# Edge rows of a four-layer graph network put together in DRAM during the attention and loaded in one piece per half chunk, with rows of 268 bytes

## The reference, cut to what matters

```python
h = relu(layernorm(x)); x = x + gnn0(h)   # attention over 4 heads, per edge; sum over dst; projection, norm
h = relu(layernorm(x)); x = x + cheb(h)   # two Chebyshev layers of order 3, rows summed by src
h = relu(layernorm(x)); x = x + gine(h)   # see below
h = relu(layernorm(x)); x = x + gat(h)    # softmax over the edges of each dst

def gine(node_feats):                      # edge_feats = edge_attr_64
    message = relu(node_feats[dst] + edge_feats)
    message_reduce = segment_sum(message, src, 3125)
    return mlp((1 + eps) * node_feats + message_reduce)
```

## Time and profile before

| | us |
|---|---|
| median of 3 runs | 3534.71 |
| lowest and highest run | 3491.54, 3550.27 |
| span of the profiled execution | 3529.8 |
| POOL busy in the 800 scatters (L1254) | 818.6 |
| first and last scatter start | 1576.7, 2938.6 |

### The profile page before, as it was taken

One profiled execution on the slowest core, in us unless ns is written; L12 is line 12 of the kernel. 1 busy time (PEld: TensorE's weight loads), 2 busy tenths in 40 slices (PEclk: granted clock), 3 DMA queues, 4 the chain that ended last, 5 costly groups with the idle time before them and its releaser, 6 DMA issues. The chain is left out here.

```text
span 3529.8 us, 59565 instructions
## 1 busy us (share of the span) xinstructions
PE 1964.1 (56%) x16222; PEld 1430.6 (41%) x16222; DVE 2235.0 (63%) x4872; ACT 1128.3 (32%) x3658; POOL 1615.5 (46%) x1665
## 2 busy tenths in 40 slices
PE   6844555555555555545766556564545445564487
PEld 5723333333333333334344435453434434554222
DVE  7877777777777777754521112134547557987899
ACT  1144555444444444533210111000001001117544
POOL 1055555555555555553666666645666562000000
PEclk9955555555555555556767677675657657985699
DMA  7912121121212222236222222215544432220000
GB/s 240 364 40 45 42 45 43 43 43 44 45 40 45 42 45 41 45 88 224 65 49 50 50 50 48 60 44 154 147 132 145 127 81 84 85 82 0 0 0 9
DMA packets 399309, 267.13 MB, mean 76 GB/s; under 512 B 321456, under 2 KB 349293, under 8 KB 399073
## 3 DMA queue, kind: packets, MB, share of 16 engines
q1 hardware_dynamic: 306278, 87.81, 11.6%
q10 hardware_dynamic: 41472, 118.96, 9.3%
q0 software_dynamic: 51488, 59.40, 6.7%
HBM read 158.59 MB, written 107.47 MB: 75 GB/s over the span
## 5 line engine op out<-in xcount | busy, mean ns | idle before, releaser
L1254 POOL DMA_INDIRECT sorted_edges<-r_load,r_to x800 | 818.6, 1023 | 544.9 <-SPq L1188 310.2
L807 POOL DMA_INDIRECT hsrc<-h,edges x808 | 775.7, 960 | 593.8 <-PE ps L1004 362.4
L1004 PE MATMUL ps<-AO,hsrc 125*64 125x64 f32 x1616 | 195.9, 316 | 309.9 <-remote 254.3
L1049 PE MATMUL ps<-hot,lo 125*128 125x400 bf16 (+2 forms) x1000 | 272.8, 455 | 100.5 <-DVE hot L866 79.9
L1004 PEld LDWEIGHTS ps<-AO,hsrc 125*64 125x64 f32 x1616 | 180.0, 224 | 345.8 <-issue 345.8
L1031 PE MATMUL ps<-rwin,there 120*125 120x256 bf16 x800 | 183.2, 404 | 235.3 <-DVE there L850 220.0
L875 DVE TENSOR_TENSOR prod<-ps,hsrc 125x1024 f32<-125x1024 f32 x200 | 244.3, 1222 | 105.1 <-issue 101.0
L1572 ACT ACTIVATE w_work<-w_work 128x384 f32<-128x384 f32 (+1 forms) x160 | 85.8, 536 | 701.5 <-DVE w_work L1773 530.4
L866 DVE TENSOR_SCALAR hot<-ramp,small 125x400 bf16<-125x400 int16 x800 | 211.9, 322 | 148.0 <-issue 142.7
L1426 PE MATMUL ps<-R 128*128 128x64 bf16 x3000 | 156.6, 218 | 184.5 <-DVE R L1762 115.9
L1031 PEld LDWEIGHTS ps<-rwin,there 120*125 120x125 bf16 x800 | 145.1, 209 | 274.1 <-issue 274.1
(11 more groups left out here) (412 smaller groups left out, 4187.1 us busy)
## 6 DMA issues: line engine op xcount, KB each, us to landing
w_work<-sorted_edges ACTq DMA_DIRECT2D x42, 1000.0 KB
r_load<-in_edge_attr_dram SPq DMA_DIRECT2D x80, 312.5 KB
dstrow<-dst_rows SPq DMA_DIRECT2D x101, 234.4 KB
sorted_edges<-A ACTq DMA_DIRECT2D x10, 2000.0 KB, 9.7
A<-counts SPq DMA_DIRECT2D x12, 1600.0 KB
counts<-A ACTq DMA_DIRECT2D x4, 4000.0 KB, 29.8
sorted_edges<-A ACTq DMA_DIRECT2D x15, 1000.0 KB, 9.5
hsrc<-h,edges POOLq DMA_INDIRECT x808
```

The source lines that it names most:

```text
L807: g.indirect_dma_start(out=hsrc[:, s, t, :], out_offset=None, in_=S.h0[:, :], in_offset=bass.IndirectOffsetOnAxis(ap=edges.bitcast(I32)[:, ...
L1004: mm = pe.matmul(sums.rearrange("d (h w) -> d h w", h=H)[:, :, OFF[t]:OFF[t] + SUB], hsrc[0:TP, s, t, :], AO[0:TP, t, :, :], start=(t == 0 ...
L1049: mm = pe.matmul(S.ps[:, at0 + c0:at0 + c1], lo[0:TP, s, t, :], hot[0:TP, t, c0 - k0:c1 - k0], start=(t == FIRST[k]), stop=False, skip_gro ...
L1254: g.indirect_dma_start(out=S.sorted, out_offset=bass.IndirectOffsetOnAxis(ap=to[:, hf, t:t + 1], axis=0), in_=load[:, hf, t, :], in_offset ...
```

## The change

In `front` DVE now writes src+1, dst+1 and pos side by side into one tile `trip` (125 x 800 x 3 words), and ACT stores it in one piece at the place of the old store of pos (1.2 MB); the early store of the pairs is gone. SP writes the three unused partitions of each half chunk in the new array `staged_edges`: zero rows once, and three small DMAs with their places. `staged_edges` is [40 chunks, 2 halves, 128, 10 rows, 67 floats].

In `attend` SP's loop is cut in two. In the first 40 pairs, after the eight loads of the pair, SP issues four DMAs from DRAM to DRAM (`stage_chunk`), which put the features (1250 pieces of 256 B per half) and the triples (1250 pieces of 12 B per half) of one chunk into their rows. In the remaining pairs there is nothing more. At the end SP waits for `settled` in place of `padded`, and POOL's memset of the load buffer is gone.

`bring_half` is one DMA of 128 x 2680 bytes, and POOL waits for 16 per half. The scatter takes its places from column D + 2 of the loaded row. A row of `sorted_edges` has 67 floats (268 bytes) in place of 80 (320), in the clears, the scatters and the loads of the items.

```diff
-ROW = D + 16
+ROW = D + 3
...
-    pairs = sb("f_pairs", [TP, K, 2], F32)[:, :, :]
-    pos_all = sb("f_pos", [P, K], I32)[:, :]
-    pos = pos_all[0:TP, :]
+    trip = sb("f_trip", [TP, K, 3], F32)[:, :, :]
+    pos = trip.bitcast(I32)[:, :, 2]
+    spare = sb("f_spare", [P, K], I32)[:, :]
...
-    STORES = 11
+    STORES = 13
...
+            sp.dma_start(S.staged[:, :, TP:P].rearrange("c h p t w -> (c h) p (t w)"),
+                         zrow[0:2 * C2, 0:HALF * ROW].unsqueeze(1).to_broadcast([2 * C2, P - TP, HALF * ROW])).then_inc(q["blank"], 16)
             sp.dma_start(S.r3[0:PAD].rearrange("n s c -> n (s c)"), zero[0:PAD, :]).then_inc(q["stored"], 16)
-            sp.wait_ge(q["pairs"], 1)
-            sp.dma_start(S.pairs.rearrange("(c p t) k -> p c (t k)", p=TP, t=TC),
-                         pairs.rearrange("p (c t) k -> p c (t k)", t=TC)).then_inc(q["stored"], 16)
+            sp.wait_ge(q["constc"], 5)
+            sp.wait_ge(q["blank"], 16)
+            with nc.allow_non_contiguous_dma(reason="the places of three rows that carry no edge, in each half chunk"):
+                for k in range(TP, P):
+                    sp.dma_start(S.staged.bitcast(I32)[:, :, k, :, D + 2:D + 3].rearrange("c h t k -> (c h) t k"),
+                                 spare[k:k + 1, :].rearrange("p (g t) -> p g t", t=HALF)).then_inc(q["stored"], 16)
             sp.wait_ge(q["stored"], 16 * STORES)
...
-            own.did(v.tensor_scalar(pairs[:, :, 0], src, 1.0, None, ALU.add))
-            own.step(v.tensor_scalar(pairs[:, :, 1], dst, 1.0, None, ALU.add))
-            v.sem_inc(q["pairs"], 1)
+            own.did(v.tensor_scalar(trip[:, :, 0], src, 1.0, None, ALU.add))
+            own.step(v.tensor_scalar(trip[:, :, 1], dst, 1.0, None, ALU.add))
...
-            act.dma_start(S.pos, pos_all).then_inc(q["stored"], 16)
+            act.dma_start(S.trip, trip.rearrange("p g k -> p (g k)")).then_inc(q["stored"], 16)
...
-def bring_half(nc, I, S, sp, c, hf):
...
-    sp.dma_start(S.to[:, hf, :], S.pos[:, bass.ds(c * TC + hf * HALF, HALF)]).then_inc(S.landed[hf], 16)
+def bring_half(S, sp, c, hf):
+
+    sp.dma_start(S.load[:, hf, :, :], S.staged[bass.ds(c, 1), hf].rearrange("c p t w -> (c p) t w")).then_inc(S.landed[hf], 16)
+
+
+def stage_chunk(nc, I, S, sp, c):
+
+    by_edge = "(p h t) f -> h p t f"
+    for hf in range(2):
+        rows = S.staged[bass.ds(c, 1), hf, 0:TP].rearrange("c p t w -> (c p) t w")
+        sp.dma_start(rows[:, :, 0:D], I["edge_attr_64"][bass.ds(c * CE, CE), :].rearrange(by_edge, h=2, t=HALF)[hf]).then_inc(S.settled, 16)
+        with nc.allow_non_contiguous_dma(reason="two node numbers and a place behind each row of features"):
+            sp.dma_start(rows[:, :, D:D + 3], S.trip[:, bass.ds((c * 2 + hf) * (HALF * 3), HALF * 3)].rearrange("p (t k) -> p t k", k=3)
+                         ).then_inc(S.settled, 16)
...
-            with sp.Fori(0, n) as j:
+            with sp.Fori(0, C2) as j:
                 for s in range(2):
-                    i = j * 2 + s
-                    g, b = begin(i, s)
-                    sp.wait_ge(q["window_free"], i + 1)
-                    sp.dma_start(rwin[:, s, :], S.r3[bass.ds(b, W)].rearrange("n s c -> (n s) c")).then_inc(q[f"rwin{s}"], 16)
-                    line(g, i)
+                    bring(j * 2 + s, s)
+                stage_chunk(nc, I, S, sp, j)
+            with sp.Fori(C2, n) as j:
+                for s in range(2):
+                    bring(j * 2 + s, s)
...
-            sp.wait_ge(S.padded, 1)
+            sp.wait_ge(S.settled, C2 * 64)
             for hf in range(2):
-                bring_half(nc, I, S, sp, 0, hf)
+                bring_half(S, sp, 0, hf)
...
-            g.memset(S.load[:, :, :, :], 0.0).then_inc(S.padded, 1)
...
-                    g.wait_ge(S.landed[hf], c * 48 + 48)
+                    g.wait_ge(S.landed[hf], c * 16 + 16)
...
-                        g.indirect_dma_start(out=S.sorted, out_offset=bass.IndirectOffsetOnAxis(ap=to[:, hf, t:t + 1], axis=0),
+                        g.indirect_dma_start(out=S.sorted, out_offset=bass.IndirectOffsetOnAxis(ap=load.bitcast(I32)[:, hf, t, D + 2:D + 3], axis=0),
```

More of the change, by code:

```diff
@@ L253, in front @@
         "oh", "rank", "htp", "ht", "r", "hi", "rem", "mid", "lo", "d16", "spans", "ends1", "jumps1", "past1", "count1", "items1",
-        "pairs", "rows", "base", "pos", "nw", "cum", "items", "stored")}
-    STORES = 11
+        "blank", "rows", "base", "pos", "nw", "cum", "items", "stored")}
+    STORES = 13
     LATE = 5
@@ L694, in _ @@
             pe.matmul(S.bank[7][:, 1:2], onesf[0:TP, :], xa[:, K - 1:K], start=True, stop=True).then_inc(q["base"], 1)
-def bring_half(nc, I, S, sp, c, hf):
-    part = slice(hf * HALF, (hf + 1) * HALF)
-    by_edge = "(p t) f -> p t f"
-    sp.dma_start(S.load[0:TP, hf, :, 0:D], I["edge_attr_64"][bass.ds(c * CE, CE), :].rearrange(by_edge, t=TC)[:, part, :]
-                 ).then_inc(S.landed[hf], 16)
-    with nc.allow_non_contiguous_dma(reason="two node numbers behind each row of features"):
-        sp.dma_start(S.load[0:TP, hf, :, D:D + 2], S.pairs[bass.ds(c * CE, CE), :].rearrange(by_edge, t=TC)[:, part, :]
-                     ).then_inc(S.landed[hf], 16)
-    sp.dma_start(S.to[:, hf, :], S.pos[:, bass.ds(c * TC + hf * HALF, HALF)]).then_inc(S.landed[hf], 16)
+def bring_half(S, sp, c, hf):
[8 more added lines that the diff above has]
+                         ).then_inc(S.settled, 16)
 def attend(nc, I, S, sb, sem):
@@ L749, in pairs_of @@
     def pairs_of(eng):
-        return eng.value_load(S.count[0:1, 1:2], min_val=1, max_val=P * IC // 2 - 1)
+        return eng.value_load(S.count[0:1, 1:2], min_val=G // 2, max_val=P * IC // 2 - 1)
     with nc.Block() as block:
@@ L1102, in spread @@
     assert NB % UN == 0
-    load, to = S.load, S.to
+    load = S.load
     GROUPS = ((0, 7), (7, 13), (13, 19), (19, NB))
@@ L1195, in both @@
                     sp.sem_inc(qr["ready"], 1)
-                    bring_half(nc, I, S, sp, c + 1, hf)
+                    bring_half(S, sp, c + 1, hf)
             def again(r):
@@ L2229, in build @@
         S.ovn = keep("ovn", [1, 8], I32)
-        S.cleared, S.tail, S.padded = (nc.alloc_semaphore(n) for n in ("cleared", "tail", "padded"))
+        S.cleared, S.tail, S.settled = (nc.alloc_semaphore(n) for n in ("cleared", "tail", "settled"))
         S.landed = [nc.alloc_semaphore(f"landed{hf}") for hf in range(2)]
@@ L2240, in build @@
         S.items2 = dram("items2", [P * IC2, 2], I32)
-        S.pairs = dram("edge_pairs", [E, 2])
-        S.pos = dram("places", [P, C2 * TC], I32)
+        S.trip = dram("edge_places", [TP, C2 * TC * 3])
+        S.staged = dram("staged_edges", [C2, 2, P, HALF, ROW])
         S.sorted = dram("sorted_edges", [SORTED + SPARE, ROW])
@@ L2250, in build @@
             S.load = sb_in(loads)("r_load", [P, 2, HALF, ROW], F32)
-            S.to = sb_in(loads)("r_to", [P, 2, HALF], I32)
             S.hpw = S.R[0:D, :]
```

7 lines of the change are left out of this document (6 added, 1 removed).

## The result

The changed kernel takes 4079.86 us (median of 4 runs, 4076.3 to 4087.63) against 3539.68 us of the kernel before in the same rounds: ratio 1.160, 95% interval 1.154 to 1.167. The forecast was 3785 us with a range of 3430 to 4060. The sign was right; the loss is 545 us of span (4074.6 - 3529.8) where 255 were forecast, and lies just outside the range.

What follows compares the result with a forecast made beforehand. No engine was full in attention; in spread, the other engines' speed beside POOL's scatters counted, and SP was to become attention's bound. 3529.8 + 244 + 7 - 6 + 10 = 3785 us, range 3430 to 4060.

Steps and rivals of the forecast that it cites:

- Part 1: Attention: four staging DMAs per pair take 10.7 us of SP, 4.6 idle, so SP becomes the bound: +244 us.
- the tail: End of attention: two one-piece loads replace six, so waits for spot and edges go: -6 us, once.
- Part 2: Front: the larger exposed store costs +8 us, the dropped memset gives -1.4: together +7 us.
- Part 4: Spread: quick loads remove POOL's stops, scatters end earlier, but other engines run slowly beside them: +10 us.
- f: Spread: fraction of full speed at which work goes beside scatters; 0.59 before, 0.46 taken after, 0.30 lowest.
- ACT at 1593.15: Spread: ACT starts promptly after PE among the first 15 scatters, taken as a sign that signals pass without stops.
- The 0.66 for the Chebyshev part: Spread: Chebyshev speed beside scatters as a fraction of full speed, from blocks of 5.33 us against 8.1 us.
- Rival B: Attention cheap, but in spread scatters without stops hold PE's signals all the time, +183: 3729 us; chance 0.11.
- Rival A: Staging hidden in attention, +0 to +30, and spread gives -124: 3422 us; chance 0.19.
- Rival C: Staging in attention: small DRAM writes take twice the time, +670, 4210 us; at 1.3 times +372, 3913 us; chance 0.12.
- Rival D: Attention +244, spread -124: 3651 us; or POOL's stop stays, spread 0; chance 0.08 for this second half and the rest.
- the hold: Spread: PE's signals are held up while POOL issues scatters in a row and let go near its stops.

Runs made afterwards that it cites:

- run with counting: Kernel before, SP counting up a semaphore 250 times after each of the first 40 attention pairs, no DMA added: 3380.43 us against 3106.97 us.
- run with the triples alone: Changed kernel staging only the 12-byte pieces, features left out, whole staged array blanked in front: 3920.35 us.
- quick loads: Kernel before, places loaded first, node pairs left out: 3746.27 us against 3540.35; on a later chip 2886.24 against 3107.78.
- both stops: Kernel before, go only after scatters land, fourth gather awaited before the fifth: 3438.62 us, ratio 0.973; on a later chip 3399.02 against 3107.78.

## Why the prediction was wrong, point by point

**Part 1 (staging, +244), right, with luck in the size.** SP became the bound, in the way that was worked out. But the four DMAs held SP 13.2 us, not 10.7, and SP could absorb some 6.5 us, not 4.6. The two errors nearly cancel: the pair grew by 6.7 us where 6.1 were forecast. With front (+8 against +7) and the tail, the first scatter came 261 us later where 245 were forecast. The run with counting shows the cause without any traffic, the run with the triples alone shows that a stage of 3.0 us goes into SP's idle time for nearly nothing.

**Part 2, right** (+8 in front).

**Part 4, wrong: "I take +10 (f = 0.46), near the middle".** This is the step that failed. Most stops gone, scatters in a row, PE held: all as described. But f came out under the lower end of what I had put (0.30). By the item loop it is 43/182 = 0.24. Over the stage, without the 279 us in which POOL stood still (1436 - 279 = 1157 us of scatters), 1867 = 1024 + 1157 (1 - f) gives 0.27. The term was +284 and not +10. With f = 0.27 and the forecast's 1060 us of scatters it would have been +215; the rest comes from the 97 us by which scatters took longer than forecast, with the stops that remained. The wait for the Chebyshev part was not in the forecast at all, so the last scatter came 1436 us after the first and not 1060; it added little to the time, since the other engines worked at full speed in it.

The rows had part of the answer. The fair value for "no stops" was the slow stretch of each period, not the mean with the fast one. The row that I weighed against it (ACT at 1593.15) was a single prompt signal, just behind a wait of ACT of 23.36 us. And 5.33 us was not the full speed of a block: with POOL silent it takes 4.3 us from 2622.42 to 2626.76 above, and 3.9 to the next one. The 0.66 for the Chebyshev part was therefore nearer to 0.5, and the stage had more to lose from slow scatters than I reckoned. Rival B had the right mechanism in spread, and its price (+183) together with the forecast's attention would have made 3958 us, inside the range; I held the two for alternatives, but they are two stages and add up.

**Rival A** (staging hidden) is out, by the pair period on every chip. **Rival C** (small DRAM writes slower than the loads) was half right, and the time fell between its 3913 and 4210 us all the same by chance. At 1.3 times the loads it had the four at 13.9 us, and they took 13.2. But its price of +372 took the idle time of 4.6 us with it, and attention lost 253 us; the rest of the loss is spread's. **Rival D** (f unchanged) is out on chips with the hold.

**What the forecast could not know:** that before's f = 0.59 holds only where the hold is. On two of the chips the hold was absent, the change was neither faster nor slower (3118 against 3126 and 3108 us), and the terms were +267 in attention and -275 in spread. The term for attention is nearly the same there as on the first chip; the one for spread has the other sign.

## What to carry to other kernels

A loop of loads on one queue has a budget: the time in which the issuing engine waits in a round. Here 3.0 us a round cost nearly nothing, and of 13.2 us about half was paid in each round, though the DMA share was only 0.39. A DMA in 1250 pieces of 256 bytes cost 3 to 4 us of the issuer here, most of it charged to the DMA behind it. Before a stop of POOL is removed, look at what the other engines do in it: here they did their work there. And when terms of a forecast lie in different stages, add the bad ends before giving a range.

## What the runs showed of the hardware that was not expected

- While POOL issued indirect DMAs 1.27 us apart, 20 and more in a row, PE started independent matmuls 0.7 us or a multiple of it apart instead of 0.17 at the same clock, and DVE's waits for PE are "remote". What counts is how often POOL stops: the item loop does 43 DVE instructions in 100 us with one stop of 4 us in 20 scatters, 104 with one of 3 to 6 us in 10, and 152 with a stop of 2.3 us after each 5; stops of 0.3 to 0.9 us brought nothing. SP shows the same step: in the kernel before an issue of dstrow takes 0.01 to 0.02 us or 0.70 (median 0.02), and where nothing is held each takes 0.33 us (820.22 in the run with counting). What they lack in that time (its instructions, or a path for its signals) no run here tells; this stays open.
- It is there in the runs on some chips and not in those on others. The kernel before took 3532 to 3606 us on three chips and 3107 to 3126 us on two. Its traces of the two kinds differ in the "remote" waits, 781 us in sum against none. A gain measured on one chip can have the other sign on the next: quick loads +6% and -7%, both stops -3% and +9%.
- Staged rows of 268 bytes and of 320 bytes made no difference to scatters and items (2236.8 and 2237.6 us from the first scatter on). The Trainium skill (DMA: Bandwidth & Descriptors, Specifications) says that transfers under 512 B are read-modify-writes below line rate. All staged pieces are under it; a piece of 256 B took 27 ns of a DMA engine from DRAM to DRAM against 18 as a load, and one of 12 B 14 ns, so there is a cost, but the smallest writes are not the dearest. Whether a read-modify-write is behind it no run here shows.
